# Layer 0's second half of tiles is combined, normalized, transposed and routed inside layer 1's turns 0 to 5

## The reference

```python
xn = _layernorm(x, axis=-1)
x = x + _L0_attn_ref(xn, ...) + _L0_ffn_ref(xn, ...)
xn = _layernorm(x, axis=-1)
x = x + _L1_attn_ref(xn, ...) + _L1_ffn_ref(xn, ...)
xn = _layernorm(x, axis=-1)
x = x + _L2_attn_ref(xn, ...) + _L2_ffn_ref(xn, ...)
xn = _layernorm(x, axis=-1)
x = x + _L3_attn_ref(xn, ...) + _L3_ffn_ref(xn, ...)
```

```python
logits = xt @ router_W + router_b
probs = jax.nn.softmax(logits / T, axis=-1)
top_p, top_i = jax.lax.top_k(probs, K)          # K = 3
cw = cw.at[jnp.arange(n)[:, None], top_i].set(top_p)
h = jax.nn.relu(jnp.einsum('nd,edh->neh', xt, eW1) + eb1)
ye = jnp.einsum('neh,ehd->ned', h, eW2) + eb2
routed = jnp.einsum('ned,ne->nd', ye, cw)
```

## Time and profile before

| what | us |
|---|---|
| median of 3 runs (lowest, highest) | 1791.4 (1785.49, 1794.98) |
| the profiled execution's own time | 1796.15 |
| its span in the trace | 1794.3 |
| PE busy (share of the span) | 1502.5 (84%) |
| DVE busy | 1149.0 (64%) |
| ACT busy | 866.6 (48%) |
| POOL busy | 445.7 (25%) |

### The profile page before, as it was taken

The page is one execution under the profiler, slowest core; times in us unless marked ns, Lnnn a source line. Parts: engine busy times, 40 slices in busy tenths (PEclk is TensorE's granted clock), DMA queues, the critical chain, the costliest instruction groups (busy, mean ns, idle before and its releaser), DMA issues.

```text
span 1794.3 us, 41191 instructions
## 1 busy us (share of the span) xinstructions
PE 1502.5 (84%) x11707; PEld 945.8 (53%) x11707; DVE 1149.0 (64%) x3266; ACT 866.6 (48%) x1971; POOL 445.7 (25%) x542
## 2 busy tenths in 40 slices
PE   5356899999998877999997478899999699999998
PEld 4112566656565355888886134455554245555554
DVE  6733566667566865666665556566667667777774
ACT  1022344444444423444442045566665268788887
POOL 3465223223222112222223521122222211000000
PEclk9996799999898858999996589999999779999999
DMA  8431344544543403233320223444442011111110
GB/s 261 127 136 58 102 152 136 175 123 148 160 129 101 116 1 130 107 141 141 129 107 21 97 65 114 135 138 138 138 138 76 21 42 52 53 50 52 47 51 12
DMA packets 127876, 184.77 MB, mean 103 GB/s; under 512 B 14657, under 2 KB 107217, under 8 KB 125345
## 3 DMA queue, kind: packets, MB, share of 16 engines
q1 hardware_dynamic: 94864, 144.54, 25.1%
q10 hardware_dynamic: 26112, 25.17, 4.8%
q0 software_dynamic: 6816, 14.02, 2.2%
HBM read 148.44 MB, written 42.84 MB: 107 GB/s over the span
## 4 chain that ended last, share of the span: by engine, by line
PE 59%; DVE 15%; issue 9%; DMA 5%; ACT 4%; POOL 4%; another core or an unknown queue 1%; SPq 1%; DVEq 1%; ACTq 0%; POOLq 0%
PE pH L528 8%; PE pO L733 7%; PE pT_ L594 6%; PE pY L541 6%; PE pH L620 6%; PE pY L628 5%; DVE mx L1339 3%; PE pS L676 3%; PE pS L698 3%; DMA stk<-packed_qk 2%; ACT pex L847 2%; PE pT_ L592 2%; POOL sorted_x L991 2%; PE pT_ L512 2%; DMA packed_qk<-qk 1%
## 5 line engine op out<-in xcount | busy, mean ns | idle before, releaser
L847 ACT ACTIVATE pex<-pT_ 128x512 f32<-128x512 f32 (+1 forms) x768 | 427.1, 560 | 495.8 <-PE pT_ L594 361.1
L1339 DVE TENSOR_REDUCE mx<-pS 128x2 f32<-128x512 f32 x512 | 347.9, 689 | 154.5 <-PE pS L571 107.5
L594 PE MATMUL pT_<-stk 32*128 32x256 f16 x1024 | 203.9, 285 | 90.9 <-DMA stk<-packed_qk 31.0
L888 POOL DMA_INDIRECT home_y<-ysb,home x117 | 115.1, 984 | 543.4 <-DVE ysb L1362 283.2
L571 PE MATMUL pS<-stk 32*128 32x256 f16 x1024 | 208.3, 291 | 27.6 <-DVEq L1082 17.6
L733 PE MATMUL pO<-pex,va 128*9 128x256 f32 (+1 forms) x3072 | 206.6, 390 | 2.6 <-ACT pex L847 2.6
L594 PEld LDWEIGHTS pT_<-stk 32*128 32x128 f16 x1024 | 55.7, 93 | 209.5 <-issue 86.4
L840 ACT ACTIVATE wb<-pH,b 128x256 f32<-128x256 f32 x256 | 107.3, 470 | 106.6 <-PE pH L528 106.2
L528 PE MATMUL pH<-XT,w 128*128 (+1 forms) x512 | 132.0, 386 | 1.1
L620 PE MATMUL pH<-xsT,wb 128*128 128x128 f32 x888 | 132.4, 294 | 0.3 <-ACT xsT L816 0.3
L851 ACT ACTIVATE pT_<-later 128x384 f32<-128x384 f32 x256 | 126.6, 494 | 8.1
(11 more groups left out here) (220 smaller groups left out, 2584.6 us busy)
## 6 DMA issues: line engine op xcount, KB each, us to landing
wb<-in_w SPq DMA_DIRECT2D x72, 514.0 KB
stk<-packed_qk ACTq DMA_DIRECT2D x96, 256.0 KB, 2.7
wb<-in_w SPq DMA_DIRECT2D x39, 578.0 KB
packed_qk<-qk SPq DMA_DIRECT2D x144, 128.0 KB, 2.0
wb<-gates_turned SPq DMA_DIRECT2D x8, 2048.0 KB, 7.0
pex<-gates_turned SPq DMA_DIRECT2D x8, 2048.0 KB, 7.1
xsb<-sorted_x SPq DMA_DIRECT2D x111, 64.5 KB, 4.1
sorted_x<-in_c_places SPq DMA_DIRECT2D x4, 1548.0 KB, 15.7
```

What stands on the lines that cost most here:

```text
L594: return pe.matmul(bank[:, part * T:(part + 1) * T], key, stk[rows, side, j, 0:T], start=True, stop=True)
L847: ins = act.activation(pex[:, k % 8, 0:n], bank[:, 0:n], ACT.Exp)
L888: pool.indirect_dma_start(YH, bass.IndirectOffsetOnAxis(ap=home[:, place_:place_ + 1], axis=0), ysb[:, place_, :], None).then_inc(sem(f"ho ...
L1339: ins = dve.tensor_reduce(mx[:, :, j, col], bank.rearrange("p (c n) -> p c n", c=2), AX.X, ALU.max)
```

## The change

Four constants set how much of a layer's preparation is done early: `EARLY[1]` is 4, so `phase_a(1)` covers groups 0 to 3 and only the first half (tiles 0 to 15) is chosen ahead of layer 1's turns; `AHEAD` is 0 everywhere, so what the code adds for it does nothing. `ADDED[0]` is 18: in layer 0's turns 14 and 15 DVE combines 18 tiles in place of 28, over the same steps. None follows behind turn 16.

The rest moves into layer 1's turns as new steps. Turns 0 to 3 have four m each: DVE combines one tile (tiles 18 to 31, then the last statistics). Turns 1 to 4 bring one group each (4 to 7): q (POOL, inverse deviation), x (DVE, normalizes four tiles), a (PE, transposes into the second bank of `pT_`, ACT copies to `XT`) and b (PE, router products, ACT copies to `LG`). Turn 5 has k0, k1 and k2, the second half's choice in three parts on DVE, with the exponents on ACT at k1; POOL waits for it at k2, two turns before the row that needs it is staged. Layer 1's loop now covers turns 6 to 13 and four more turns are written out. `row_stats` has a buffer of its own (`rs6`).

```diff
+GROUPS = NT // 4
+
+
+AHEAD = {0: 0, 1: 0, 2: 0, 3: 0}
+EARLY = {0: GROUPS, 1: 4, 2: GROUPS, 3: 8}
+ADDED = {l: min(4 * EARLY[l + 1] + 2, 2 * (B - 2)) for l in SORTED}
+AHEAD_FROM = B + 1 - AHEAD[2]
+CHOICES = {}
+if EARLY[1] < GROUPS:
+    CHOICES[GROUPS - EARLY[1] + 1] = (1, 1)
+if AHEAD[2]:
+    CHOICES[B - 1] = (2, 0)
...
-LOOPS = {0: (2, 12), 1: (2, 14), 2: (2, 14), 3: (2, 14)}
+LOOPS = {0: (2, 12), 1: (6, 14), 2: (2, 14), 3: (2, 14)}
...
-        frame = ["F"] + when(behind, ("B", 0)) + when(here, ("Z", 0)) + ["F"] * 3 + when(here and behind, ("e", 0))
-        frame += when(ahead, ("G", 0)) + ["F"]
-        frame += when(here, ("N", 0)) + ["F"] * 4 + when(ahead, ("R", 0)) + ["F"] * 3 + when(here, ("A", 0))
+        added, turned = EARLY[1] + n, GROUPS + EARLY[1] + n - 1
+        adds, turns = here and added < GROUPS, here and GROUPS + EARLY[1] <= turned < 2 * GROUPS
+        add = lambda part: when(adds, ("m", 4 * added + 2 + part))
+        if AHEAD_FROM <= n:
+            turned, turns = 2 * GROUPS + n - AHEAD_FROM, True
+        chooses = n in CHOICES
+        frame = when(turns, ("q", turned)) + ["F"] + when(behind, ("B", 0)) + when(here, ("Z", 0)) + ["F"] + add(0)
+        frame += when(turns, ("x", turned)) + ["F"] * 2 + when(here and behind, ("e", 0)) + when(chooses, ("k", 0))
+        frame += when(ahead, ("G", 0)) + add(1) + ["F"]
+        frame += when(here, ("N", 0)) + ["F"] + when(turns, ("a", turned)) + ["F"] + add(2) + ["F"]
+        frame += when(chooses, ("k", 1)) + ["F"] + when(ahead, ("R", 0)) + ["F"] + when(turns, ("b", turned)) + ["F"]
+        frame += add(3) + when(chooses, ("k", 2)) + ["F"] + when(here, ("A", 0))
...
+            def turn_late(l, g):
+
+                pe.wait_ge(sem("xn_ready"), PRIMED + l * GROUPS + g + 1)
+                pe.wait_ge(sem("logits_copied"), PRIMED + l * GROUPS + g)
+                for u in range(4):
+                    ins = pe.transpose(pT_[:, 1, u * P:(u + 1) * P], XN[:, 4 * g + u, 0:P], ident[:, :])
+                ins.then_inc(sem("turned"), 1)
+
+            def logits_late(l, g):
+
+                pe.wait_ge(sem(f"ld_{l}"), full[f"ld_{l}"])
+                pe.wait_ge(sem("xts_ready"), PRIMED + l * GROUPS + g + 1)
+                for u in range(4):
+                    t = 4 * g + u
+                    ins = pe.matmul(pT_[:, 1, u * 16:u * 16 + EXPERTS[l]], XT[:, t * P:(t + 1) * P], wr[l][:, :],
+                                    start=True, stop=True)
+                ins.then_inc(sem("logits"), 1)
...
+                    elif kind == "a":
+                        turn_late(*divmod(k, GROUPS))
+                    elif kind == "b":
+                        logits_late(*divmod(k, GROUPS))
...
-                pe.wait_ge(sem("xts_ready"), PRIMED + (l + 1) * (NT // 4))
+                pe.wait_ge(sem("xts_ready"), PRIMED + l * GROUPS + EARLY[l])
...
+                if l < 3 and early < GROUPS:
+                    exponents(l, 0)
...
+                    elif kind == "a":
+                        g = k % GROUPS
+                        act.wait_ge(sem("turned"), PRIMED + k + 1)
+                        act.activation(XT[:, g * 4 * P:(g + 1) * 4 * P], pT_[:, 1, :], ACT.Copy)\
+                           .then_inc(sem("xts_ready"), 1)
+                    elif kind == "b":
+                        of, g = divmod(k, GROUPS)
+                        act.wait_ge(sem("logits"), PRIMED + k + 1)
+                        act.activation(LG[:, g * 4:g * 4 + 4, 0:EXPERTS[of]],
+                                       pT_[:, 1, 0:64].rearrange("p (u e) -> p u e", e=16)[:, :, 0:EXPERTS[of]],
+                                       ACT.Copy).then_inc(sem("logits_copied"), 1)
+                    elif kind == "k" and k == 1:
+                        exponents(*CHOICES[turn.n])
...
+                        elif kind == "q":
+                            inverse_deviation(*divmod(k, GROUPS))
+                        elif kind == "k" and k == 2 and CHOICES[turn.n][0] == 1:
+                            pool.wait_ge(sem("gates_late"), 1)
...
+            def normalize(l, g):
+                dve.wait_ge(sem("rstd"), PRIMED + l * (NT // 4) + g + 1)
+                for t in range(4 * g, 4 * g + 4):
+                    ins = dve.tensor_scalar(XN[:, t, 0:P], X[:, t, :], MV[:, t, 0:1], rstd[:, t:t + 1],
+                                            ALU.subtract, ALU.mult)
+                ins.then_inc(sem("xn_ready"), 1)
...
-                in_turns = 2 * (B - 2)
+                in_turns = ADDED[l]
...
+                    elif kind == "m":
+                        combine(l - 1, *added[l - 1], (k,))
+                    elif kind == "q" and k >= 2 * GROUPS and l == 1:
+                        dve.sem_inc(sem("stats"), 1)
+                    elif kind == "x":
+                        normalize(*divmod(k, GROUPS))
+                    elif kind == "k":
+                        of, part = CHOICES[turn.n]
+                        dve.wait_ge(sem(f"ld_{of}"), full[f"ld_{of}"])
+                        choose(of, part, (k,))
+                        if k == 2 and of == 1:
+                            dve.sem_inc(sem("gates_late"), 1)
...
-                    choose(l, 0)
+                    if not AHEAD[l]:
+                        choose(l, 0)
                 if l == 1:
-                    routing(l)
-                if l == 1:
-
+                    if EARLY[l] == GROUPS:
+                        choose(l, 1)
+                    chain.link(dve.memset(GA[:, :, 15:16], 1.0))
+                    dve.sem_inc(sem("gates"), 1)
...
-                if l in SORTED:
-                    combine(l, final, stats, range(2 * (B - 2), NT + 2))
+                    dve.sem_inc(sem("stats"), GROUPS - AHEAD[2])
+                if l in SORTED and EARLY[l + 1] == GROUPS:
```

83 lines of the change are left out of this document (43 added, 40 removed).

## The result

| | kernel before | changed kernel |
|---|---|---|
| median (lowest to highest), 20 runs each | 1791.46 us (1778.64 to 1802.08) | 1785.81 us (1775.89 to 1804.88) |
| ratio, 95% interval | | 0.996 (0.9943 to 0.9977) |

By the ratio the change takes about 7 us off (by the medians 5.7), where 14.7 was forecast: 1776.7. The time lies inside the range (1765 to 1788), but within 0.5% of the kernel before, a case that had a chance of 0.23. By the mean of the four ratios the gain is 9.6 us, two thirds of what was forecast.

The account below looks back on a forecast made before the run. PE was taken to bound layer 1's turns, DVE to be the fuller engine in layer 0's last turns. Terms -11.9 - 18.7 + 16.0 = -14.6 us off the profiled 1796.15 gave 1781.5; 4.75 lower against the median, 1776.7 us; range 1765 to 1788.

Parts of the forecast that it names:

- Part 2: Between layers 0 and 1: of 40.1 us, 18.7 go and 21.4 stay, with four groups left at half clock.
- rival C: Cheaper: the four groups between the layers run at full clock, or the x wait vanishes; 1770 us, chance 0.08.
- Part 1: Layer 0's last turns: 18 combined tiles in place of 28 shorten 44.9 us to 33.0, a gain of 11.9 us.
- sign of being wrong: The prediction is wrong if Part 1 saves under 6 us, or turns 0 to 5 together cost more than 22.
- rival A: The clock still falls in layer 0's turn 15, so Part 1 gives 5.8 us; 1782.9 us, chance 0.10.
- Part 3: Layer 1's turns 0 to 5 take on the moved work at a cost of 16.0 us, bounds 6.2 and 32.
- PE's work: Layer 1's turns 1 to 4: transposes and router products of a group cost PE 1.55 us, 6.2 for four.
- The wait before the transposes: Layer 1's turns 1 and 2: PE waits about 0.8 us for DVE's tile and normalization, with the hand-over.
- Turn 0: Layer 1's turn 0: four tiles on DVE, no PE work, slack of 1.0 us plus idle time; cost 0.5 us.
- Turn 5: Layer 1's turn 5: the choice's 7.6 us, all ahead of H7's gating, less waits and slack; cost 5.5 us.
- rival D: Slower: turn 5's pause drops PE to clock 0.50, 16.3 us per turn, two such turns giving 1809 us; chance 0.06.
- Rival B: DVE's queue in layer 1's turns is fuller, gatings are slowed by POOL; Part 3 costs 24, 1784.8 us, chance 0.14.

Follow-up runs that it names:

- fill: Changed kernel plus PE products without a reader: 10 ahead of the transposes between layers 0 and 1, 36 behind, 10 in turn 0; 1780.20 us, 0.9959.
- nothing added at V: Without 3 products without a reader ahead of each V product in layer 0's turn 14; the changed kernel with only these took 1752.02 us, 0.9937.
- adds put back: Changed kernel with 28 tiles again combined in layer 0's turns 14 and 15, all else as changed; 1757.55 us, 0.9972 of the kernel before.
- change again: The changed kernel measured again without an edit; 1753.63 us, 0.994 of the kernel before.
- spreading: Changed kernel, choice moved behind last gatings of turns 4 to 6, two of each turn's four tiles behind its last gating, transposes one piece later; 1749.88 us, 0.991.
- Everything spread and filled: Changed kernel with choice and tiles spread, six tiles ahead of turn 0's first gating, and PE products without a reader; 1760.97 and 1736.42 us, 0.985 and 0.9856.
- products at V: Everything spread and filled, plus 3 products without a reader ahead of each V product in layer 0's turn 14; 1762.24 us, 0.9855 of the kernel before.
- filled: First measurement of everything spread and filled; 1760.97 us, 0.985 of the kernel before.
- filled again: Second measurement of everything spread and filled, without an edit; 1736.42 us, 0.9856 of the kernel before.

## Why the prediction was right and wrong

**Part 2 was right.** 21.4 us were to stay; ten traces of the changed order without fill in the gap show 20.95 to 21.40, where before it was 40.13. The four groups ran at half clock, as taken (in one trace, the 20.95, the first four transposes were still at full clock, 0.63 us). That it could be otherwise (rival C's first reason) took the fill to show.

**Part 1 named the right mechanism with the wrong weight.** Its step "I take layer 2's time plus the 1.7 us that DVE has more: 33.0 us. Gain 44.9 - 33.0" took the kernel before from one trace, 22 us of it at half clock, and the changed one at full clock, and put the whole difference down to ten tiles. At full clock on both sides the tiles are worth 5.9 us (36.74 against 30.85, of the 9.8 us that DVE spends on ten tiles). The rest is the clock: from V to end, four traces of the kernel before show 40.3 to 43.5 us (mean 42.4), and four of the changed kernel 30.8 to 41.5 (mean 33.8). That is 8.6 us in place of 11.9. With every trace that has 28 tiles (five, mean 41.3) and every one with 18 and nothing added at V (eleven, mean 33.3) it is 7.9. The 33.0 itself was near: counted from the first add, as the prediction did, the four traces of the changed kernel give 33.9 in the mean, as a mixture of 31 to 32 and 41.7. Too large was what it was taken from. The 44.9 is the longest of the four traces of the kernel before (mean 43.8), and 1.2 us of the difference is the mark: with 28 tiles the first add comes 1.39 us ahead of V, with 18 only 0.14. By the shown pair of traces the first part saved 2.0 us, under the 6 that the prediction had named as its sign of being wrong. That rival A ("the clock still falls") stood beside the forecast as an alternative was a fault too: both happen in one kernel, from execution to execution, and the fall begins in turn 14, not in turn 15.

**Part 3 was too cheap.** Turns 0 to 5 take 123.7 us in the mean of four traces, against 104.2 in the mean of two: 19.5 for 16.0, and turn 6 1.3 more. Term by term:

- PE's work: 1.55 a group was taken, 1.34 measured (turn 4). The router's products follow the clock almost whole, 0.96 us to their modelled end, some 0.81 to the next product, against 1.73 at half clock. The Trainium skill (TensorE: Matmul & The Clock Gate, LDWEIGHTS), by which I had worked out 0.86, was nearer than my 1.0. Its formula has no term for the clock. In turn 1, at full clock, the router's weight loads (L558) start 0.11 us apart, as its 107 ns has it; at half clock 0.21.
- The wait before the transposes: 0.8 taken, 0.49 measured; before Y6 and Y7 0.6 taken, 0.42 + 0.49 measured in turn 1. Turns 1 and 2 came to 3.5 each in place of 3.0. The walk put the first wait down to a tile and the normalization together; with the adds put back, turn 1 has the normalization without a tile, and no wait. "Less since later steps have small gaps too" was the weak step: the tiles cost 2.1 us of DVE's 4 in turn 1. Turns 3 and 4 came out cheaper than taken, 2.0 and 1.3 for 2.4 and 1.6.
- Turn 0: 0.5 taken, 2.7 measured (mean 25.35 against 22.67). "The end of its turn has the slack of 1.0 plus idle time" was read from turn 1. In turn 0 all gatings start late, behind the gates' transfer, so there was no slack. Without tiles (adds put back) the turn is 22.86 us, and PE waits 2.14 us ahead of Y0 and not at all ahead of Y6 and Y7; with them ("change again", the same set) it is 24.76, and the waits are 2.93, 0.74 and 0.49 us. That is 2.0 us more of waiting for 1.9 us more of turn. The half clock behind the wait at Y0 is not new: the kernel before has a wait of 2.88 us there and four products at 2.08 us behind it; where the wait is longer (3.64 us in the trace shown) the half clock lasts longer, and the waits at Y6 and Y7 vanish. The rows, first of "adds put back" and then of "change again":

```profile
642.60 1.23 PE L581 MATMUL pY<-wb,w 128*128 128x256 f32 x4 [2.14 <-DVE wb L1450]
```

```profile
635.77 2.07 PE L581 MATMUL pY<-wb,w 128*128 128x256 f32 x4 [2.93 <-DVE wb L1450]
...
647.38 1.13 PE L581 MATMUL pY<-wb,w 128*128 128x256 f32 x4 [0.74 <-DVE wb L1450]
649.00 1.13 PE L581 MATMUL pY<-wb,w 128*128 128x256 f32 x4 [0.49 <-DVE wb L1450]
```

- Turn 5: 5.5 taken, 6.5 measured, 2.70 + 2.37 us of it waits, 0.95 of the rest the last four products at half clock (2.08 for 1.13). This is rival D, begun and cut short: it cost turn 6 1.3 us, not 16.3 for each of two turns. The clock was back within turn 6. The rule of the Trainium skill behind D (same page, Why this matters for your kernels), that a pause throws the engine back to half clock, agrees with what happened here and in turn 0. What it costs is another matter: with PE full behind the pause, it was some us and not whole turns.
- Turn 8: nothing taken, 0.3 measured, in every trace of this kernel and in the kernel before with its turns written out. The prediction costs the written-out turns at nothing; turns 0 to 7 bear that out, turn 8 does not.

Rival B (24 us in part 3) came as near to the 20.8 us of turns 0 to 6 as the forecast's 16.0, but not by its reason: the gatings were not slowed, they take 0.73 to 0.75 us in the mean in turns 1 to 3 where they took 0.76 to 0.78 before, and what was found are waits for gatings that stand behind moved steps.

With the measured terms the sum is -8.6 - 18.8 + 19.5 + 1.3 + 0.3 = -6.3 us; the four ratios say -7.2, -10.6, -7.3 and -13.4, mean -9.6. The difference of 3 us is inside what the unexplained parts of the runs move. The steps that failed are terms of the sum that were read from one row each. The length of layer 0's end came from one execution and one mark (11.9 us taken, 8.6 measured), and turn 0's slack from turn 1 (0.5 taken, 2.7 measured): together 5.5 of the 8.3 us by which the sum was too large. The rest is turns 1, 2 and 5 (1.0 and 1.0 us more than taken), turns 6 and 8 (1.6, taken as nothing), less 0.7 in turns 3 and 4.

**What stays open.** Why the clock falls in layer 0's turn 14 in some executions and not in others (the Trainium skill, TensorE: Matmul & The Clock Gate, What's actually happening, says that the clock gate's timing does not start anew with a kernel, which would fit; no run here tests it); and why medians and stages part: spreading gains 11 us in the stages and 4 in the medians, fill 3 and none, and both together 16.1 and 14.7 against the unaltered change in their sets (1778.38 to 1762.24, 1751.13 to 1736.42), near what their stages give (16 and 19). The places outside the marked stages move by 7 to 10 us each from one trace to another: layer 0 from its first attention add to V 431 to 440 us, layer 2 from its first to its last attention add 336 to 343, and from there to the end of the kernel 386 to 395. No run here separates them.

**A better version.** Everything spread and filled runs at 0.985 to 0.9856 of the kernel before in three measurements (one of them with products at V too; 5 or 6 runs each), 25 to 28 us less, and beats the changed kernel as well.

## What to carry to other kernels

A step that is moved under a full engine costs what its place in the other engine's queue makes it cost: the same 7.6 us of choice cost 6.5 us ahead of the last gatings and nothing behind the last gatings of three turns, where DVE waits for the next turn anyway. Slack must be read from the very turn that gets the work, and a stage that holds stretches of half clock needs several executions before a difference is put down to the work in it.

## What the runs showed of the hardware

- PE's standing ahead of the groups between the layers bears on their clock. After a wait of 2.93 us it was at half from the first group (in one trace of the changed kernel from the second) and stayed there to the last, although PE was hardly idle; with the wait cut to 0.73 us by ten products they began at full clock (four transposes in 0.63 to 0.66 us, a group's router products in 0.96). After a wait of 4.56 us it was at half from the second four transposes on.
- The clock can also fall within such a run of transposes and 15-column products with PE busy throughout (0.51 from 634 to 636 in "filled", behind 2.00 of 2.00 us busy). It did in three of the four traces of the changed order with these products, at different places, and not in "filled again".
- The same code with the same waits runs at either clock: layer 0's end took 31.00 us at 1.00 in one execution and 41.70 at 0.67 in another, with PE's waits of 0.55 and 0.70 us in both.
- A router weight load (128 columns, f32) follows the clock: the next starts 0.11 us later at full clock (turn 1 of the changed kernel) and 0.21 at half.
- The kernel before takes 1764 us on two of the chips and 1789 on two others. In the changed kernel's traces the difference lies ahead of layer 0's first V product (573 and 580 us on the former, 595 on a latter, and 1177 to 1178 us behind it in all three), and nearly 20 us of it ahead of layer 0's first attention add (140 and 141 us against 160). What makes it stays open.
